# Score bound, term loads, tail weights and the tail's routing chain placed elsewhere

## The reference, cut to what matters

```python
x = x + L0_attn(layernorm(x))     # linear attention with exponential features
x = x + L0_ffn(layernorm(x))      # soft mixture of 16 experts
x = x + L1_attn(layernorm(x))     # softmax attention
x = x + L1_ffn(layernorm(x))      # top-2 mixture of 32 experts

def L1_attn(x):                   # x: (4, 2048, 256), 16 heads of 16
    q, k = rotary(x @ Wq.T), rotary(x @ Wk.T); v = x @ Wv.T
    scores = einsum('bhqd,bhkd->bhqk', q, k) * Dh ** -0.5      # causal
    return einsum('bhqk,bhkd->bhqd', softmax(scores), v) @ Wo.T

def L1_ffn(x):
    rw = softmax(x @ router_w.T)               # 32 experts
    vals, idx = top_k(rw, 2)
    return sum over e of (x * w_e[:, None]) @ W_e   # w_e: vals where e was chosen, else 0
```

## Time and profile before

| | us |
|---|---|
| median of 3 runs | 2872.36 (2869.97 to 2879.84) |
| profiled execution | 2871.75 |
| its span | 2870.0 |
| busy in the span: PE, ACT, DVE, POOL | 2451.6, 1794.2, 1571.8, 733.9 |
| bound: DVE's first to last instruction | 1283.81 to 1296.40 |
| attention: first turn to last product of PE | 1302.91 to 2318.67 |
| tail: first projection to the end | 2334.66 to 2870.0 |

### The profile page before, as it was taken

The page is one execution under the profiler, slowest core; times in us unless marked ns, Lnnn a source line. Parts: engine busy times, 40 slices in busy tenths (PEclk is TensorE's granted clock), DMA queues, the critical chain, the costliest instruction groups (busy, mean ns, idle before and its releaser), DMA issues. The chain is left out here.

```text
span 2870.0 us, 63297 instructions
## 1 busy us (share of the span) xinstructions
PE 2451.6 (85%) x24666; PEld 1410.1 (49%) x24666; DVE 1571.8 (55%) x2607; ACT 1794.2 (63%) x2682; POOL 733.9 (26%) x1006
## 2 busy tenths in 40 slices
PE   6888898886688889857999999999999977789872
PEld 3545555453567656532333333334333356567751
DVE  5767768577775567645445554444555338520233
ACT  3443535343565435437999999999999933356420
POOL 2203021120000047731121212112121103454465
PEclk9999999998899899978999999999999988799986
DMA  7800000001100024464756667665667334478767
GB/s 256 273 26 1 1 1 1 1 1 27 20 1 1 1 63 157 147 135 91 123 102 106 136 116 124 116 112 102 114 128 119 52 98 151 158 258 268 253 225 241
DMA packets 251996, 308.83 MB, mean 108 GB/s; under 512 B 100544, under 2 KB 180160, under 8 KB 251584
## 3 DMA queue, kind: packets, MB, share of 16 engines
q1 hardware_dynamic: 237344, 269.49, 40.0%
q0 software_dynamic: 12288, 33.57, 3.4%
q10 hardware_dynamic: 2080, 1.84, 0.2%
HBM read 157.23 MB, written 147.59 MB: 106 GB/s over the span
## 5 line engine op out<-in xcount | busy, mean ns | idle before, releaser
L1790 ACT ACTIVATE at_PT<-at_pS 128x1024 f32<-128x1024 f32 (+2 forms) x1152 | 1002.5, 1236 | 10.8 <-PE at_pS L1817 10.7
L1648 POOL TENSOR_SCALAR_AFFINE_SELECT at_PT<-at_PT 128x256 f32<-128x256 f32 (+1 forms) x384 | 194.4, 515 | 825.7 <-ACT at_PT L1790 825.4
L1817 PE MATMUL at_pS<-hd_QT,hd_KT 99*32 99x512 bf16 (+3 forms) x5120 | 318.9, 351 | 7.0 <-DVE at_QT L1762 4.8
L1817 PE MATMUL at_pS<-at_QT,at_KT 99*32 99x512 bf16 (+3 forms) x5120 | 315.7, 348 | 2.8 <-issue 1.1
L1738 DVE COPY at_OT<-at_pO 128x512 f32<-128x512 f32 x64 | 44.3, 692 | 476.3 <-PE at_pO L1835 471.6
L1835 PE MATMUL at_pO<-at_PT,at_V 128*32 128x512 f32 (+3 forms) x2560 | 289.6, 529 | 4.3 <-issue 4.1
L1835 PE MATMUL at_pO<-at_PT,hd_V 128*32 128x512 f32 (+3 forms) x2560 | 289.1, 529 | 0.1
L2378 PE MATMUL tl_bank<-tl_W,tl_xT 128*128 x896 | 240.0, 406 | 27.1 <-issue 25.0
L1817 PEld LDWEIGHTS at_pS<-hd_QT,hd_KT 99*32 99x32 bf16 x5120 | 113.7, 95 | 263.9 <-ACT at_PT L1790 169.6
L1817 PEld LDWEIGHTS at_pS<-at_QT,at_KT 99*32 99x32 bf16 x5120 | 114.1, 95 | 256.9 <-ACT at_PT L1790 164.8
L451 ACT ACTIVATE la_ft<-la_ft 128x1024 f32<-128x1024 f32 x128 | 135.2, 1056 | 161.3 <-DVE la_ft L274 161.1
(11 more groups left out here) (353 smaller groups left out, 4152.6 us busy)
## 6 DMA issues: line engine op xcount, KB each, us to landing
tl_xin<-rows_in SPq DMA_DIRECT2D x56, 512.0 KB
rows_out<-tl_yout SPq DMA_DIRECT2D x56, 512.0 KB
score_terms<-at_parts SPq DMA_DIRECT2D x60, 384.0 KB, 5.6
rows_in<-la_zeros SPq DMA_DIRECT2D x8, 2048.0 KB, 7.6
rotated_qk<-qk_qkT SPq DMA_DIRECT2D x16, 1024.0 KB, 4.3
at_qk<-rotated_qk SPq DMA_DIRECT2D x60, 256.0 KB, 4.4
rows_in<-la_zeros SPq DMA_DIRECT2D x4, 3072.0 KB, 11.4
values<-qk_rv SPq DMA_DIRECT2D x64, 192.0 KB, 4.6
```

The costliest lines, as they stand in the source:

```text
L1648: nc.gpsimd.affine_select(out=d, in_=d, compare_op=ALU.is_ge, fill=0.0, base=0, pattern=of, channel_multiplier=-1).then_inc(masked, 1)
L1790: nc.scalar.activation(PT[u % 6][:, 0:banks, 0:width], pS[u % 3][:, 0:banks, 0:width], ACT.Exp, scale=HD ** -0.5).then_inc(exp_done, 1)
L1817: last = mm(pS[u % 3][r:r + 32, b, col:col + 512 - off], KT[par][0:KS, h, kb * P + r:kb * P + r + 32], QT[par][0:KS, h, c * 512 + off:(c + ...
```

## The change

The bound's instructions go to the end of the projection stage's lists: DVE's behind its last `sums`, ACT's root behind its last copy, PE's three behind its last turn. They use PSUM tiles of the projections. The block bd, and the clearing of its semaphores, go. The twelve term loads go in three groups of four, behind the qkT stores of quads 12, 13 and 14. SP's wait for first_out stands behind the qkT store of quad 12. ACT writes two rows of ones behind quad 14 and two behind quad 15. Wo and R are loaded by SP in attention, behind the shifts, into the place of the projections' weights, which stays allocated to the end. In the tail the sum of the router's columns and Rc stand behind the first projection and addition; `less` stands behind the addition of x = 5, `places(0)` and `places(1)` behind the additions of pairs 15 and 31.

```diff
-            sp.wait_ge(first_out, 32)
-            sp.sem_inc(ones_free, 1)
-            store(3, lambda q: load_terms(sp, keep, 0, keep["QT0"], keep["KT0"], slice(0, N), first_out, range(3 * q, 3 * q + 3)))
+            def first_terms(q):
+                if q == 0:
+                    sp.wait_ge(first_out, 32)
+                    sp.sem_inc(ones_free, 1)
+                if q < 3:
+                    load_terms(sp, keep, 0, keep["QT0"], keep["KT0"], slice(0, N), first_out, range(4 * q, 4 * q + 4))
+            store(3, first_terms)
...
+            dve.drain()
+            v.memset(ones[:, :], 1.0)
+            for b in range(B):
+                v.tensor_reduce(km[:, b * H:(b + 1) * H], k2[:, b * TPB:(b + 1) * TPB, :].rearrange("p t h -> p h t"), AX, ALU.max)
+            dve.drain().then_inc(km_ready, 1)
+            dve.wait_ge(km_turned, 1)
...
-                if q >= NQ - 4:
-                    if q == NQ - 4:
-                        act.wait_ge(ones_free, 1)
-                    h = q - (NQ - 4)
-                    nc.scalar.activation(keep["KT0"][KR:KS, h, :], mean[KR:KS, 0:1].broadcast_to([KS - KR, N]), ACT.Copy, scale=0.0, bias=1.0)
+                if q == NQ - 2:
+                    act.wait_ge(ones_free, 1)
+                if q >= NQ - 2:
+                    for h in range(2 * (q - NQ + 2), 2 * (q - NQ + 2) + 2):
+                        nc.scalar.activation(keep["KT0"][KR:KS, h, :], mean[KR:KS, 0:1].broadcast_to([KS - KR, N]), ACT.Copy, scale=0.0, bias=1.0)
             for f in range(4):
                 square(NQ - 1, f)
                 empty(NQ - 1, NQ // 2 - 1, 1, f)
+            act.wait_ge(squared, 1)
+            nc.scalar.activation(bd[:, :, :], bd[:, :, :], ACT.Sqrt).then_inc(rooted, 1)
...
+            pe.wait_ge(zT_ready, NT + 2)
+            pe.wait_ge(v_ready, NT + 2)
             pe.wait_ge(km_ready, 1)
-            nc.tensor.transpose(pK[:, :], km[:, :], ident[:, :]).then_inc(km_turned, 1)
+            nc.tensor.transpose(pK, km[:, :], ident[:, :]).then_inc(km_turned, 1)
...
+                sp.dma_start(keep["Wo"], io["WoT"].rearrange("(c p) n -> p c n", p=P)).then_inc(tail_loaded, 16)
+                sp.dma_start(keep["R"], io["routerT"].rearrange("(c p) n -> p c n", p=P)).then_inc(tail_loaded, 16)
...
             for p in range(NP):
                 add(p)
+                if p == 0:
+                    dve.wait_ge(made, 6)
+                    v.tensor_copy(code[:, :], codei[:, :])
+                    v.tensor_copy(col[:, :], coli[:, :])
+                    dve.wait_ge(summed, 1)
...
                     if x == 4:
                         count(b)
+                    if x == 5:
                         less(b)
                 if p == 14:
                     offsets(0)
+                if p == 15:
                     places(0)
...
                 if p == 30:
                     offsets(1)
+                if p == 31:
                     places(1)
```

More of the change, by code:

```diff
@@ L1152, in project_qkv @@
     FIRST = NQ // 2
+    nmax, need_max = keep["nmax"], keep["need_max"]
+    BH = B * H
+    km, kcol, dg = mem.sb("km", [P, BH]), mem.sb("kcol", [BH, 1]), mem.sb("dg", [BH, BH])
+    ones = mem.sb("ones", [BH, P])
+    bd = mem.sb("bd", [P, NT, H])
+    gap, worst, over = mem.sb("gap", [P, 1]), mem.sb("worst", [1, 1]), mem.sb("over", [1, 1])
+    km_ready, km_turned, dg_ready, spread, squared, rooted, gap_ready, gap_turned = (mem.sem(n) for n in (
+        "km_ready", "km_turned", "dg_ready", "spread", "squared", "rooted", "gap_ready", "gap_turned"))
+    pK, pM, pG = pT[0][0:BH, 0, :], pT[1][:, 0, 0:BH], pV[0][0:1, 0:P]
+    q2, k2, own = (nn[:, :, n * H:(n + 1) * H] for n in range(3))
     first = keep["QT0"][:, 0:2, :].rearrange("p h n -> p (h n)").bitcast(fp32)
@@ L1247, in _ @@
             quad(NQ + 1, sums)
+            dve.drain()
[4 more added lines that the diff above has]
+            dve.wait_ge(km_turned, 1)
+            v.tensor_reduce(kcol[:, :], pK, AX, ALU.max)
+            dve.drain()
+            v.tensor_scalar(dg[:, :], ident[0:BH, 0:BH], kcol[:, 0:1], None, ALU.mult).then_inc(dg_ready, 1)
+            dve.wait_ge(spread, 1)
+            for b in range(B):
+                last = v.tensor_tensor(bd[:, b * TPB:(b + 1) * TPB, :], q2[:, b * TPB:(b + 1) * TPB, :],
+                                       pM[:, b * H:(b + 1) * H].unsqueeze(1).broadcast_to([P, TPB, H]), ALU.mult)
+            last.then_inc(squared, 1)
+            dve.wait_ge(rooted, 1)
+            for b in range(B):
+                for g in range(G):
+                    v.tensor_scalar(nmax[:, b * G + g, :, :].rearrange("p h t -> p t h"),
+                                    bd[:, b * TPB:(b + 1) * TPB, g * 4:g * 4 + 4], -1.0, ROOM, ALU.mult, ALU.add)
+            dve.drain()
+            v.tensor_tensor(bd[:, :, :], bd[:, :, :], own, ALU.subtract)
+            dve.drain()
+            v.tensor_reduce(gap[:, :], bd[:, :, :].rearrange("p t h -> p (t h)"), AX, ALU.max).then_inc(gap_ready, 1)
+            dve.wait_ge(gap_turned, 1)
+            v.tensor_reduce(worst[:, :], pG, AX, ALU.max)
+            dve.drain()
+            v.tensor_scalar(over[:, :], worst[:, :], LOOSE, None, ALU.is_lt)
+            dve.drain()
+            v.tensor_scalar(over[:, :], over[:, :], -1.0, 1.0, ALU.mult, ALU.add)
+            dve.drain()
+            v.tensor_copy(need_max[:, :], over[:, :])
         @block.gpsimd
@@ L1457, in _ @@
+            pe.wait_ge(zT_ready, NT + 2)
+            pe.wait_ge(v_ready, NT + 2)
             pe.wait_ge(km_ready, 1)
[L1458 removed]
+            nc.tensor.transpose(pK, km[:, :], ident[:, :]).then_inc(km_turned, 1)
             pe.wait_ge(dg_ready, 1)
[L1460 removed]
+            nc.tensor.matmul(pM, ones[:, :], dg[:, :], start=True, stop=True).then_inc(spread, 1)
@@ L1461, in _ @@
             pe.wait_ge(gap_ready, 1)
-            nc.tensor.transpose(pG[:, :], gap[:, :], ident[:, :]).then_inc(gap_turned, 1)
+            nc.tensor.transpose(pG, gap[:, :], ident[:, :]).then_inc(gap_turned, 1)
 TERMS_Q = (0, 0, 0, 1, 1, 2)
@@ L2379, in multiply @@
                 last.then_inc(multiplied, 1)
-            pe.wait_ge(small_loaded, 32)
-            pe.wait_ge(made, 6)
-            for c in range(DC):
-                last = mm(pC[:, 0:E1], ones[:, :], R[:, c, :], start=(c == 0), stop=(c == DC - 1))
-            last.then_inc(summed, 1)
             for n in range(NP + 2):
@@ L2388, in _ @@
                     project(n)
+                if n == 0:
+                    pe.wait_ge(made, 6)
+                    for c in range(DC):
+                        last = mm(pC[:, 0:E1], ones[:, :], R[:, c, :], start=(c == 0), stop=(c == DC - 1))
+                    last.then_inc(summed, 1)
                 if 1 <= n < NP + 1:
@@ L2458, in build @@
             stage("qk", project_qkv, io, keep, nn, st)
-            stage("bd", bound_scores, io, keep, nn)
             own.close()
```

80 lines of the change are left out of this document (11 added, 69 removed).

## The result

| | before | after |
|---|---|---|
| median, us | 2872.36 (7 runs, 2869.97 to 2881.74) | 2860.64 (7 runs, 2853.78 to 2865.43) |
| ratio | | 0.995, interval 0.9934 to 0.9965 |
| profiled execution | 2871.75 | 2864.33 |
| its span | 2870.0 | 2862.6 |

The change makes the kernel 0.5% faster: 11.7 us by the medians, where 19.0 were forecast (2853.4 us). The time lies inside the range and outside the likeliest case's own range (2849.5 to 2858). That the median falls on its number is luck.

The account below looks back on a forecast made before the run. At the projections' end SP's term loads and DVE's independent bound run one after the other. 15.45 + 7.5 - 3.3 - 1.9 + 0.2 + 1.0 = 18.95 us gives 2853.4 us as median, range 2843 to 2865 us.

Parts of the forecast that it names:

- the likeliest case: Whole kernel: all terms summed give 2853.4 us, own range 2849.5 to 2858 us, chance 0.52.
- The bound: End of projections: bound starts at DVE's own end, not at 1283.81 us, taking out 15.45 us of idle time.
- the middle part: Projections from z0 to the end of the last sums: V0, fourth loads and rows of ones, together +2.3 us.
- V0: Projections, ahead of quad 13: ACT's stand for V0's load moves and value runs earlier, +7.5 us (2.7 to 11.1).
- The fourth load: Projections: one more 256 KB load costs 1.64 us by rate; two quads pay it, -3.3 us (0 to -6.0).
- the bound with SP's issue: Upper limit for one more term load: 2.03 us plus its issue of 0.95 us in SP's queue, 3.0 us.
- The rows of ones: End of ACT's projections: two rows instead of one stand ahead of the last squares, -1.9 us.
- The tail's start: 288 KB less ahead of the head outputs, worth 0.3 us; with SP's issue and column sums, +0.2 us.
- The links: Tail's routing chain in shorter pieces: PE enters the expert products earlier, +1.0 us (-1.5 to +5.5).
- The 5.46 us: Tail: addition of pair 31 and PE's entry into the expert products 5.46 us earlier, lost by group 1's first rows.
- the +1.0: Tail: gain taken for the shorter routing links, +1.0 us, bounds -1.5 and +5.5 us.
- Rivals 3 and 4: Tail's gathers: late instructions add 18.5 us each (one 0.07, two 0.03); or miss the burst, 2834.9 us (0.08).

Follow-up runs that it names:

- e1_bound: Kernel before with only the bound's instructions moved into the projections' lists; ratio 0.995 to before, 12.4 us faster by medians.
- e12_paced: Changed kernel with POOL's scatters of group 1 paced by the expert products from the first on; ratio 0.9957 to before, 12.2 us faster.
- e3_tail: Kernel before with the tail's parts alone (Wo and R in attention, column sums moved, links); ratio 0.9997 to before, 0.9 us faster.
- e4_after: The changed kernel run again, on chip 12, for a second trace; ratio 0.9946 to before, 12.0 us faster.

## Why the prediction was right, and where it was not

- **The bound.** Right: 15.3 us of idle time gone, SP waits at the end of the stage and not the others, same length. With the loads left at the end, SP is through 1.7 us behind DVE (e1_bound), so taking them away was needed for the whole. The first instruction of the bound is at 1274.04 us, 1270.0 without the late start, where 1266 was named: that is the middle part. By e1_bound this one term is all of the gain. The 0.9 us of a shorter way to attention was not forecast.
- **V0.** Right: first value of quad 13 6.9 us earlier, at 1209.4 us when the 4.0 us ahead of z0 are taken off (1209.5 was named), 7.5 us taken. The further 3.24 us of the tile that follows at once didn't come: at the next qkT store the gain is 6.6 us.
- **The fourth load.** Mis-sized: 2.4 us each, 4.8 for 3.3. The rate of 12.69 us for 1984 KB gave 1.64 us; the bound with SP's issue (3.0 us) was nearer. The stretch of 12.69 us held latencies and waits that no byte more would lengthen, and others that one would, so its mean rate is no price of a load; that is my reading, and no run parts the two. Two stands of some 8 us were named: they are 10.63 and 6.67 us, the second with two rows of ones (3.70 us) ahead of it.
- **The rows of ones.** Right: 1.8 us for 1.9.
- **Missed**: 1.8 us between a stand's end and the next qkT store, where ACT now waits for PE's value projection (2.38 us in quad 14). The cause isn't settled, and 1.5 us of it is no more than this stretch differs between traces of one program (6.6 to 8.2 us).
- Together the middle part is 2.3 forecast and -1.5 measured: 0.6 by V0, 1.5 by the loads, 1.8 by what was missed. That is half of the distance of 7.3 us to the medians.
- **The tail's start.** Too low: the first addition comes 2.2 us earlier, and the same in each kernel with this part (18.8 to 19.0 us against 20.6 to 21.1). SP's issue of chunks to PE's first projection is 5.72 us before and 4.53 after, so the 288 KB ahead of it were worth 1.2 us and not 0.3.
- **The links.** The 5.46 us do end by the first rows of group 1, as forecast, and the size of POOL's delay was short: 2.7 us for 1.45. SP's load of those rows was to go out 0.8 us earlier and goes out 2.6 us later (239.4 against 236.8 us from the first addition); behind it the two traces are equal (294.7 and 295.1 us). So the +1.0 had the wrong sign. The reason given for the end, that SP then waits for the scatters, is so on chip 12 only. On the result's chip SP waits 7.3 us for ACT's copy there, as it did before (7.4), and its load goes out 7.4 us behind the start of the last scatter in both traces, where e12_paced and chip 12 have 2.5. The sign that I named, PE waiting for the first rows of group 1, is in e3_tail (12.49 us) and not in the trace of the result.
- **Rivals 3 and 4** spoke of packets of instructions that come late, and said that one lies in the stretch of the stands of 12.79 and 5.75 us. It doesn't: the stands are from 2726.4 to 2745.5 us, and the packets next to them start at 2718.6 and 2757.6 us. What ends the first is again a late count of PE's, 14.5 us behind the recorded end of its product. The stands did move with the change: in the gathers they are 6.29, 8.50 and 6.51 us after, in group 0 the longest is 11.38 us where it was 5.91. But e4_after, the same program on chip 12, has the same 196 packets and no such stand at all, and e12_paced ties them to rows of 22 and 24 unbroken scatters, not to a place in the program. Why the counts are late on the slower chips and not on chip 12 stays open.
- The remaining -2.8 us in attention: lengths from 1006.1 to 1009.7 us stand beside each other in kernels with and without the change, so it is scatter, as are the 4.0 us at the start. They are why this one trace shows less than the medians. Of the 18.95 us forecast, 14.2 are left without them: 3.8 lost in the middle part, 2.0 in the tail, and 1.1 won around the bound. The 2.5 us from there to the medians' 11.7 are in no stretch that I can name.

## What to carry to other kernels

When transfers and a piece of computing that don't need each other run one after the other because a stage ends between them, the idle time in front of the second is a price that can be read off: 15.3 of 15.45 us went away here, and 14.1 to 15.2 of them reached the next stage. When a store that frees a buffer is queued behind loads that nobody waits for yet, change their order before their number: the same bytes behind the stores took 10 us off a stage in which one load more or less moved 2.4. And before an engine is let ahead, look for the one that it can't pass; 5 us and 19 us of PE's advance both ended at POOL's last scatter. Where the profile names no engine for a wait, look at what the instruction waits for in the program and when that semaphore changed, before a reason is given: the two rivals with the largest prices rested on a stand that was misread.

## What the runs showed of the hardware

The same kernel takes 2872 to 2879 us on chips 0 and 15 and at the result, and 2829 us on chip 12, and nearly all of it lies behind the last addition of the tail: 402.25 us in after against 359.83 in e4_after, the same program. PE's granted clock explains at most 12 of these 42 us: in that stretch it is 0.87 and 0.91, and PE is busy 286.2 and 274.2 us.

The counts differ. In the four traces of chip 12 every recorded change of a semaphore by PE, ACT or DVE stands within 0.1 us of the end of the instruction that makes it. In the ten others that is so up to the tail, and then 201 to 236 instructions of each trace have no recorded change within 1 us behind their end. All of these lie between POOL's first indirect DMA and 1 us behind its last. The count that ends ACT's longest stand is 10.75 us late in after and 14.5 us in before. With the late counts come ACT's stands and POOL's pauses, and the first 32 scatters of group 1 take 45.2 to 45.6 us in before and after and 39.9 to 40.4 us on chip 12. Each chip number stands for one set only, so that it is the chip is inferred; why it is so, no run here tells.

In a queue of SP's, 256 KB more ahead of a value store cost it 2.4 us, twice, where the stretch's mean rate gives 1.64; and the order alone took a stand of 10.63 us down to 2.12.
